# One 512-column product for a projection in place of four of 128 columns, in a decoder layer on one core

## The reference

```python
x = x + self_attention(layernorm(x), Wq, Wk, Wv, Wo)          # window of 64, causal
x = x + cross_attention(layernorm(x), ctx, ctx, mask, ...)    # q = x Wq^T + bq, k, v from ctx
x = x + ffn(layernorm(x))
# ffn: xk = mu_k*x + (1-mu_k)*x_prev ; k = relu(xk W_k^T)**2
#      out = sigmoid(xr W_r^T) * (k W_v^T)
```

## Time and profile before

| what | value |
|---|---|
| time, median of 3 runs | 896.49 us (888.1 to 898.86) |
| span of the profiled execution (first to last instruction) | 880.4 us |
| PE busy with MATMUL | 676.6 us, 77% of the span, 13,293 instructions |
| PE busy with LDWEIGHTS | 555.9 us, 63%, 13,293 instructions |
| DVE, ACT, POOL busy | 465.6, 439.7, 456.8 us |
| mean granted TensorE clock | 0.842 of full speed |
| DMA, mean over the span | 107 GB/s |

### The profile page before, as it was taken

The page is one execution under the profiler, slowest core; times in us unless marked ns, Lnnn a source line. Parts: engine busy times, 40 slices in busy tenths (PEclk is TensorE's granted clock), DMA queues, the critical chain, the costliest instruction groups (busy, mean ns, idle before and its releaser), DMA issues.

```text
span 880.4 us, 31487 instructions
## 1 busy us (share of the span) xinstructions
PE 676.6 (77%) x13293; PEld 555.9 (63%) x13293; DVE 465.6 (53%) x815; ACT 439.7 (50%) x667; POOL 456.8 (52%) x709
## 2 busy tenths in 40 slices
PE   2357765879778788879688877979898979887683
PEld 2345654667657677668567665868686767665462
DVE  6675353647545456547455454747575656451410
ACT  3042543646546475637455454737574746544230
POOL 7213533255646465755636564565756545644415
PEclk9677887989879799979889798979998989885655
DMA  4753555456545556654656555574757563323000
GB/s 118 98 89 60 104 153 95 139 95 152 96 104 128 108 130 126 140 114 119 96 128 121 106 112 107 139 115 126 129 154 118 133 104 96 101 62 101 10 25 12
DMA packets 86077, 93.81 MB, mean 107 GB/s; under 512 B 16034, under 2 KB 76532, under 8 KB 82868
## 3 DMA queue, kind: packets, MB, share of 16 engines
q1 hardware_dynamic: 85940, 91.81, 49.6%
HBM read 53.32 MB, written 37.40 MB: 103 GB/s over the span
## 4 chain that ended last, share of the span: by engine, by line
PE 44%; DMA 19%; POOL 10%; DVE 8%; issue 8%; SPq 7%; ACT 4%; POOLq 0%; DVEq 0%; ACTq 0%
DMA ck_stack<-ck_scr 14%; PE csums L509 6%; PE proj L302 5%; POOL xn L931 5%; DMA qk_stack<-qk_scr 4%; PE score_exp L494 4%; PE proj L324 4%; SPq L779 4%; PE score_max L368 3%; PE proj L528 3%; PE proj L537 3%; ACT cprobs L1179 2%; PE proj L468 2%; PE sums L433 2%; PE score_max L381 2%
## 5 line engine op out<-in xcount | busy, mean ns | idle before, releaser
L1455 DVE TENSOR_REDUCE cneg_max<-score_max 128x8 f32<-128x616 f32 x128 | 102.0, 797 | 123.4 <-PE score_max L478 123.1
L1179 ACT ACTIVATE cprobs<-score_exp 77x1024 f32<-77x1024 f32 x128 | 129.8, 1014 | 63.3 <-PE score_exp L494 61.7
L931 POOL TENSOR_SCALAR xn<-x,mean,root 128x128 f32<-128x128 f32 x192 | 151.3, 803 | 6.5 <-POOL root L923 6.2
L1455 DVE TENSOR_REDUCE neg_max<-score_max 128x8 f32<-128x1024 f32 (+1 forms) x96 | 117.0, 1219 | 44.2 <-PE score_max L381 27.1
L1179 ACT ACTIVATE probs<-score_exp 128x1024 f32<-128x1024 f32 x96 | 98.0, 1021 | 41.2 <-PE score_exp L399 34.0
L908 POOL TENSOR_TENSOR both<-stats 128x8 f32<-128x8 f32 x48 | 10.2, 212 | 191.1 <-DVE stats L1387 191.1
L478 PE MATMUL score_max<-ck_stack,cq_stack 51*128 51x77 bf16 x1024 | 44.0, 211 | 61.6 <-DMA ck_stack<-ck_scr 58.5
L509 PE MATMUL csums<-cprobs,cv_heads 77*32 77x128 f32 x2048 | 88.2, 303 | 2.5 <-ACT cprobs L1179 2.5
L478 PEld LDWEIGHTS score_max<-ck_stack,cq_stack 51*128 51x128 bf16 x1024 | 27.8, 102 | 76.8 <-DMA ck_stack<-ck_scr 62.6
L302 PE MATMUL proj<-ident,xn 128*128 128x128 f32 x192 | 37.7, 327 | 45.1 <-POOL xn L931 36.7
L494 PE MATMUL score_exp<-cq_stack,ck_stack 53*77 53x128 bf16 x1024 | 60.7, 242 | 11.5 <-ACT cprobs L1179 5.9
(11 more groups left out here) (142 smaller groups left out, 1435.9 us busy)
## 6 DMA issues: line engine op xcount, KB each, us to landing
qk_stack<-qk_scr SPq DMA_DIRECT2D x32, 384.0 KB
cq_stack<-cq_scr SPq DMA_DIRECT2D x64, 192.0 KB, 4.1
qk_stack<-qk_scr SPq DMA_DIRECT2D x32, 256.0 KB
ck_stack<-ck_scr SPq DMA_DIRECT2D x64, 122.7 KB
qk_scr<-q_parts SPq DMA_DIRECT2D x16, 384.0 KB, 2.8
qk_scr<-k_parts SPq DMA_DIRECT2D x16, 384.0 KB, 2.9
cq_scr<-cq_parts SPq DMA_DIRECT2D x16, 384.0 KB, 3.4
x<-in_x_dram SPq DMA_DIRECT2D x16, 256.0 KB, 3.3
```

What stands on the lines that cost most here:

```text
L931: nc.gpsimd.tensor_scalar(xn[n][:, b, :], src[:, b, :], mean[n][:, b:b + 1], root[n][:, b:b + 1], ALU.subtract, ALU.mult).then_inc(ln_out[ ...
L1179: nc.scalar.activation(dst, src, ACT.Exp).then_inc(exp_done, 1)
L1455: nc.vector.tensor_reduce(dst, src, AX_X, ALU.max, negate=True).then_inc(max_taken, 1)
```

## The change

The four-fold loop in `project` and the one in `mix_key` each become one product of 512 columns. The weights, the banks, the waits, the semaphores and the order of the groups stay as they are.

```diff
-            def project(dst, w, src, n):
-                for b in range(QB):
-                    last = nc.tensor.matmul(dst[:, n * b:n * b + n], wT[:, w, :], src[:, n * b:n * b + n],
-                                            start=True, stop=True)
-                return last
+            def project(dst, w, src):
+                return nc.tensor.matmul(dst[:, :], wT[:, w, :], src, start=True, stop=True)
...
-                project(bank(("k", q), (k_left, q + 1)), SK, xnT, T).then_inc(k_made, 1)
+                project(bank(("k", q), (k_left, q + 1)), SK, xnT[:, :]).then_inc(k_made, 1)
...
-                project(bank(("q", q), (q_left, q + 1)), SQ, xnT, T).then_inc(q_made, 1)
+                project(bank(("q", q), (q_left, q + 1)), SQ, xnT[:, :]).then_inc(q_made, 1)
...
-                project(bank(("cq", q), (cq_left, q + 1)), CQ, xcT, T).then_inc(cq_made, 1)
+                project(bank(("cq", q), (cq_left, q + 1)), CQ, xcT[:, :]).then_inc(cq_made, 1)
...
-                for b in range(QB):
-                    last = nc.tensor.matmul(dst[:, T * b:T * b + T], wT[:, FK, :], mixed[:, 1, b, :],
-                                            start=True, stop=True)
-                last.then_inc(fk_made, 1)
+                project(dst, FK, mixed[:, 1].rearrange("p b t -> p (b t)")).then_inc(fk_made, 1)
```

## The result

The changed kernel takes 881.46 us (median of 20 runs, 869.85 to 898.95); the kernel before, on the same chips, takes 890.92 us (20 runs, 880.24 to 905.07). Ratios here are made from undisturbed runs, so they can differ a little from the ratio of two medians. The forecast, 887 on a median of 896.49, is a ratio of 0.989. The profiled span is 871.2 us (forecast 870.9), against 880.4; the run that left this profile took 873.31 us.

The account below looks back on a forecast made before the run. PE was taken as the bound (44% of the chain), with halts at late fetches of its code blocks. Terms of -1.5, -5.5 and -2.5 us summed to -9.5: 896.5 to 887 us, 8-in-10 range 868 to 904.

Parts of the forecast that it names:

- The cause: On PE: halts come when its next 256-instruction code block arrives late behind half-1 read traffic; a halt costs 7.1 us.
- 194 + 256n: PE instruction numbers where halts without a wait begin; halts at other numbers would mean the blocks aren't the cause.
- Refills neutral: Rival: code refills stay as costly or weren't the cause, only PE's own time changes; 895 us, chance 0.22.
- PE's own time: 64 projections on PE: 0.04 us saved each at full clock, about half on the path; -1.5 us.
- Loads exposed: Rival: PE's weight loads in the projections aren't hidden, so dropping them saves 46 us; 850 us, chance 0.03.
- The blocks: PE's moved code-block borders in the steady steps: 6.2 halts instead of 7, at 7.1 us each; -5.5 us.
- The first stretch: Ahead of quad 3: quad 1's border moves from 455 to 307, ahead of the read, ending its halt; -2.5 us.
- The 16.1 us between span and median: Gap between the profiled span of 880.4 us and the median, which the forecast assumed would stay.
- Which borders halt: Sign in the steady steps: long steps at quads 3, 4, 5, 6, 8, 10, short ones at 7 and 9.
- places 316 to 515: Instructions counted from a step's first cross-key projection; borders here ask for code while the half-1 read fills the DMA engines.
- fewer than five of the eight: Mark for the eight borders in the dangerous stretch: if fewer than five halt PE, the forecast number is wrong.

Follow-up runs that it names:

- experiment 2: Changed kernel with 12 instructions of already-met waits behind each long product, restoring the old instruction count and block borders: 895.12 us, ratio 0.9998.
- experiment 3: Changed kernel with 24 tiny products per steady step ahead of the cross maxima of half 1, restoring the old step length: 891.68 us, ratio 1.0021.
- control in 6: Changed kernel with the half-1 read split into DMAs issued one after another's landing, plus 24 tiny products per step: 873.17 us, against 871.04 without them.
- experiments 1 and 4: Borders moved by waits (kernel before: 970.38, 1011.6 us; changed: 1042.36) or by tiny products (kernel before: 898.86, 920.32; changed: 885.25).
- experiment 5: Half-1 read's three DMAs issued one after another's landing, on SP alone: kernel before 870.18 us (0.9797), changed kernel 871.04 us (0.9802).
- second kernel of experiment 1: Kernel before with 70 instructions of already-met waits per steady step and every border at place 440: 1011.6 us, ratio 1.1381.

## Why the prediction was right

**The cause: right.** Five things show it. Halts begin at 194 + 256n again, and the packets of code come one per block. With long products and the old numbering the halts stand at all nine old numbers (experiment 2). Long products on a step of the old length lose the whole gain (experiment 3, with its control in 6). The place of the border alone is worth some 30 us in one pair and 10 to 21 us in another (experiments 1 and 4). And SP's order alone, with no matmul changed, gives 2.0% while PE waits no less for data (experiment 5). "Refills neutral" would have left experiment 5 at 1.00. One result stands against it, the 13.6 us between long and short products at place 306, and it isn't explained.

**PE's own time: the size not shown.** The pair of passes takes 1.12 us and at half clock nothing is saved, as worked out. That half of the saving lies on the path is not shown: with the halts mostly gone, long products are 0.9 us above short ones, so the -1.5 us can't be told from nothing. That the products themselves carry the measured 11.7 us (1.3% of 891) is excluded there. "Loads exposed" is refuted by the pair's 1.12 us: it wanted 0.8.

**The blocks: the sum right, its factors wrong.** For the ten steps the prediction had 0.8 halts fewer at 7.1 us each, -5.5 us. There are no fewer, seven before and seven after. They are shorter, 2.8 us in the mean against 4.0, which was not forecast, and that is 8.9 us less of halts with 8.0 us less of time: about 0.9 us for 1 us of halt, where 7.1 for 4.0 is 1.8. The difference between mean long and mean short steps, from which the price was taken, held more than the halt. So the term of the blocks came out near its number by shorter halts and not by fewer, and that is luck. The first stretch gained 5.8 us where 2.5 were forecast, with a second halt gone besides that of quad 1, and the end gave 4.6 us back that were not in the sum.

No single price of a halt comes out of the runs. Over the whole program 13.1 us less of halts went with 9.2 us less of span, 0.7 us for 1 us. With the split read, 29.1 us less of gaps went with 18.2 us less of span, 0.6, but the read's own delay of 13.0 us is in that. Experiments 1 and 3 have more time than their gaps account for. All these are single profiles of kernels whose runs spread by 10 to 30 us.

**The 16.1 us between span and median: no fixed cost.** In the runs on record the time of an execution is 1.8 to 3.2 us above its own span (873.31 and 871.2 us for the profile after). The 16.1 us were mostly the distance of one short execution from the median. That the span came out at 871.2 us where 870.9 was forecast is therefore chance; the ratio, 0.987 against 0.989, is what the forecast can be held to.

**Which borders halt: wrong.** The prediction had long steps at quads 3, 4, 5, 6, 8 and 10 and short ones at 7 and 9. Long are 4, 6, 7, 8 and 10. Of the eight borders in places 316 to 515 only three halted PE for 1.8 us or more (470 in quad 4, 450 in quad 6, 410 in quad 10). The other four halts came from borders at 568 (quad 7), 528 (quad 11), 36 (quad 9) and one late in quad 8's step. By the prediction's own mark, "fewer than five of the eight", the number should have been wrong; it held since halts elsewhere took their place. At one and the same place (440 in the second kernel of experiment 1) the packet of code started 2.4 to 9.6 us after PE had begun the block, over the eleven full steps. A place says where a border can hurt, not that it will. Quad 1 went as said: its halt of 2.36 us is gone (one of 1.0 us stands there now), and the first stretch is 5.8 us shorter.

**What stays open.** What decides the delay of one packet at a given place was not tried. The 4.6 us that the end of the program gives back have no halt of 1.8 us or more in the trace to go with them, and I found no cause. What else than the halts themselves makes experiments 1 and 3 as slow as they are was not traced, nor why long products at place 306 had fewer gaps than short ones. That the spread between runs of one kernel (29 us after) is the chance of the halts is a guess.

## What to carry to other kernels

An edit that changes the number of instructions on the busiest engine also moves its code-block borders, and that can outweigh the edit: here the projections' own time gave nothing that can be measured, and the 1.3% came with the moved borders. Where the trace shows "issue" in the middle of a group, number the instructions and look at the instruction queue; then spread the data traffic at that place instead of trimming the engine's work. To judge an edit of the work itself, first suppress the halts in both kernels (here by splitting a read), since otherwise the borders decide the comparison.

## What the runs showed of the hardware

A wait that is already met takes about 106 ns of PE's time (7.41 us for 70 instructions in a row), so it is no free filler. A load with a product of 64 rows and 8 columns comes closer to one: such pairs stand 32 ns apart in the trace of experiment 3, and 24 of them a step changed 871.04 us to 873.17, within the spread. And a read split into three parts that wait for each other, 10.04 us on SP's queue instead of 1.07, made the kernel faster by 2.0%: the gaps at the borders of PE's code fell from 39.3 to 10.2 us, more than the 13.0 us by which PE waited longer for that read. PE's code came in packets of 16 KB, one for each 256 instructions, and in the kernel before six of 107 started only when PE had begun the last instruction that it had.
